# Two soft-MoE feed-forwards around an attention stage, fp32 in parts: a DMA pair moved ahead of a store, the last dispatch by halves, and first parts and slot outputs made earlier and on another engine

## The reference

```
x = x + 0.5 * ffn(layernorm(x))
x = x + attn(layernorm(x))
x = x + 0.5 * ffn(layernorm(x))
```

```
x = layernorm(x, norm_g, norm_b);  se = layernorm(slot_embeds) * scale
logits   = einsum("bnd,esd->bnes", x, se)
dispatch = softmax(logits, over tokens n);  combine = softmax(logits, over all 1024 slots)
slots = einsum("bnd,bnes->besd", x, dispatch)
gate  = gelu(einsum("besd,edf->besf", slots, Wg) + bg);  up = einsum(..., Wu) + bu
eout  = einsum("besf,efo->beso", gate * up, Wd) + bd
out   = einsum("bns,bso->bno", combine, eout)
```

## Time and profile before

| | us |
|---|---|
| median of 3 runs | 1966.77 |
| lowest, highest | 1964.76, 1971.29 |
| profiled execution, its own time | 1972.29 |
| its span | 1970.6 |
| PE busy in it | 1826.4 (93%) |
| DVE, ACT, POOL busy | 1333.0, 1128.0, 830.8 |
| mean granted TensorE clock | 0.978 |

### The profile page before, as it was taken

The page is one execution under the profiler, slowest core; times in us unless marked ns, Lnnn a source line. Parts: engine busy times, 40 slices in busy tenths (PEclk is TensorE's granted clock), DMA queues, the critical chain, the costliest instruction groups (busy, mean ns, idle before and its releaser), DMA issues. The chain is left out here.

```text
span 1970.6 us, 35473 instructions
## 1 busy us (share of the span) xinstructions
PE 1826.4 (93%) x11720; PEld 1632.3 (83%) x11720; DVE 1333.0 (68%) x2397; ACT 1128.0 (57%) x2233; POOL 830.8 (42%) x1005
## 2 busy tenths in 40 slices
PE   1999999999999899959999969999999999989999
PEld 1878787888899899948999957887878889989998
DVE  5866566664788888835555458666666648888886
ACT  1666566556555677724434427565665655557775
POOL 1353433524676455412222213535343356654553
PEclk9999999999999899979999979999999999999999
DMA  2543234323465577721221136324332516546774
GB/s 65 214 171 150 96 149 150 122 96 115 156 212 173 177 257 261 263 81 53 69 71 64 43 112 251 141 95 160 138 145 85 177 57 220 199 153 229 259 263 162
DMA packets 106666, 298.20 MB, mean 151 GB/s; under 512 B 16257, under 2 KB 56321, under 8 KB 94273
## 3 DMA queue, kind: packets, MB, share of 16 engines
q1 hardware_dynamic: 106560, 296.88, 42.5%
HBM read 187.63 MB, written 109.22 MB: 151 GB/s over the span
## 5 line engine op out<-in xcount | busy, mean ns | idle before, releaser
L115 POOL TENSOR_TENSOR pool_carrier<-minus_half 128x1 f32<-128x1 f32 x220 | 59.3, 270 | 640.8 <-PE f1bank L845 165.7
L688 ACT ACTIVATE f1r_lt<-f1bank,slot_shift 128x512 f32<-128x512 f32 x128 | 88.0, 688 | 138.0 <-PE f1bank L816 138.0
L688 ACT ACTIVATE f2r_lt<-f2bank,slot_shift 128x512 f32<-128x512 f32 x128 | 88.1, 688 | 136.5 <-PE f2bank L816 136.4
L547 DVE TENSOR_TENSOR f1r_e_lo<-f1bank,f1r_e_hi 128x512 fp32r<-128x512 f32 x128 | 82.8, 685 | 88.4 <-ACT f1r_e_hi L770 88.3
L547 DVE TENSOR_TENSOR f2r_e_lo<-f2bank,f2r_e_hi 128x512 fp32r<-128x512 f32 x128 | 82.5, 685 | 85.4 <-ACT f2r_e_hi L770 85.0
L1470 PE MATMUL f1bank<-f1c_eo,f1c_e_hi 128*128 128x258 f32 (+1 forms) x512 | 132.5, 290 | 3.4 <-DVE f1c_eo L1387 3.4
L1470 PE MATMUL f2bank<-f2c_eo,f2c_e_hi 128*128 128x258 f32 (+1 forms) x512 | 131.5, 288 | 3.5 <-DVE f2c_eo L1387 3.4
L1471 PE MATMUL f1bank<-f1c_eo,f1c_e_hi 128*128 128x256 f32 (+1 forms) x512 | 130.6, 286 | 0.0
L1471 PE MATMUL f2bank<-f2c_eo,f2c_e_hi 128*128 128x256 f32 (+1 forms) x512 | 129.6, 284 | 0.0
L1342 POOL TENSOR_TENSOR f1c_e_lo<-f1c_lt,f1c_e_hi 128x512 fp32r<-128x512 f32 x64 | 83.0, 1297 | 94.0 <-ACT f1c_e_hi L1441 93.9
L1342 POOL TENSOR_TENSOR f2c_e_lo<-f2c_lt,f2c_e_hi 128x512 fp32r<-128x512 f32 x64 | 83.1, 1298 | 91.9 <-ACT f2c_e_hi L1441 91.8
(11 more groups left out here) (319 smaller groups left out, 6637.1 us busy)
## 6 DMA issues: line engine op xcount, KB each, us to landing
logits<-f1r_lt SPq DMA_DIRECT2D x16, 2048.0 KB, 7.3
f1c_lt<-logits SPq DMA_DIRECT2D x32, 1024.0 KB, 7.3
...
```

Of the source, the lines that this page charges most:

```text
L115: pool.tensor_tensor(c["pool_carrier"][:, col:col + 1], c["minus_half"][:, 0:1], c["minus_half"][:, 0:1], ALU.add)
L547: dve.tensor_tensor(e_lo[t % 2][:, h * BANK:(h + 1) * BANK], ps_t[h][:, :], rd(e_hi[t % 2][:, h * BANK:(h + 1) * BANK]), ALU.subtract).the ...
L688: act.activation(lt[:, g, sc, :], ps_l[sc % 2][:, :], ACT.Identity, bias=c["slot_shift"][:, sc:sc + 1]).then_inc(logit_out, 1)
```

## The change

1. SP, route: the DMA pair of the reciprocals (L388, L391) stands ahead of `store_xn` of the group two later, where both belong to the last group of a batch.
2. PE, route: the last two token tiles of the last batch are dispatched as (t2, h0), (t3, h0), (t2, h1), (t3, h1) instead of tile by tile, and a wait for `e_lo` is left out at the last tile.
3. ACT makes `hi_g` and `hi_u` of the second expert (`second_gate_up`) ahead of the last slots' shifts. DVE makes `lo_g` of the second expert and `in_lo` of the first (`first_in_lo`) between the two halves of the last scaling.
4. DVE, experts: `in_lo` of the next expert stands behind the four gated products instead of ahead of them. In the last expert the first shifts of the combine stage stand among the gated products, and the rows of expert 14 behind the third shift.
5. PE, experts: the last pair is written out behind the loop, with `first_spread` ahead of the last hidden products.
6. Combine: the first slot outputs, hi and lo, are made by POOL, seven of the eight ahead of its part in the stage, instead of by ACT and DVE.
7. An unused semaphore is left out.

The core of the diff:

```diff
@@ route, SP
-                if fill and exists(b, g, 2):
-                    store_xn(i + 2, g % 2, b + (g + 2) // NG, (g + 2) % NG)
                 if drain and g == NG - 1:
 
                     sp.wait_ge(inv_done, b)
...
                     sp.dma_start(inv_rows[:, :], inv_dram.rearrange("(a n) -> a n", a=1).to_broadcast([P, SL]))\
                       .then_inc(inv_loaded, DMA)
+                if fill and exists(b, g, 2):
+                    store_xn(i + 2, g % 2, b + (g + 2) // NG, (g + 2) % NG)
@@ route, DVE, in the loop over halves h of the scaling
+                            if h == 0 and not fill:
+                                experts.first_in_lo(dve)
@@ route, ACT, ahead of the last slots' shifts
+        act.wait_ge(e_tr, 1 + HB * GT * B * NG)
+        experts.second_gate_up(act)
@@ route, PE
-                        pe.wait_ge(e_lo_done, 1 + HB * (GT * j + t + 1))
+                        if not (not fill and g == NG - 1 and t == GT - 1):
+                            pe.wait_ge(e_lo_done, 1 + HB * (GT * j + t + 1))
...
-                        dispatch(b, g, j, t)
+                        if not fill and g == NG - 1 and t >= GT - 2:
+                            if t == GT - 2:
+                                pe.wait_ge(xs_done, 1 + GT * j + t + 1)
+                                dispatch_half(b, g, j, t, 0)
+                            else:
+                                pe.wait_ge(xs_done, 1 + GT * j + t + 1)
+                                dispatch_half(b, g, j, t, 0)
+                                dispatch_half(b, g, j, t - 1, 1)
+                                dispatch_half(b, g, j, t, 1)
+                        else:
+                            dispatch(b, g, j, t)
@@ experts
+    def second_gate_up(act):
+        act.wait_ge(gate_up_loaded[1], 2 * DMA)
+        for n in "gu":
+            act.activation(hi[n][1][:, :, :], raw[n][1][:, :, :], ACT.Copy).then_inc(gate_up_hi, 1)
...
+    def first_in_lo(dve):
+        gate_parts_lo(dve, 1, 1)
+        slots_lo(dve, 0, 0)
@@ experts, DVE
-                if not (last and q == 1):
-                    parts_lo(e + 1, 1 - q)
+                if not (last and q == 1) and not (first and q == 0):
+                    gate_parts_lo(dve, e + 1, 1 - q)
+                if first and q == 0:
+                    slots_lo(dve, e + 1, 1 - q)
...
+                    if last and q == 1 and f < 2:
+                        combine.first_shifts(dve, f, f + 1)
+                if not (last and q == 1) and not (first and q == 0):
+                    slots_lo(dve, e + 1, 1 - q)
                 dve.wait_ge(h_hi_done, e + 1)
...
-                if not (first and q == 0):
+                if not (first and q == 0) and not (last and q == 1):
                     rows_out(e - 1, pair - 1 + q, 1 - q)
...
-        combine.first_shifts(dve)
+        combine.first_shifts(dve, 2, 3)
+        rows_out(E - 2, E // 2 - 1, 0)
+        combine.first_shifts(dve, 3, 4)
         rows_out(E - 1, E // 2 - 1, 1)
@@ combine, POOL
+        def first_slot_out(sc):
+            pool_wait(pool, c, experts["eout_done"], 1 + 2 * B * (sc + 1))
+            pool.tensor_scalar(eo[:, 0, sc, 0:D], eout[:, 0, sc, :], 1.0, 0.0, ALU.mult, ALU.add).then_inc(eo_hi_first, 1)
+            pool.wait_ge(eo_hi_first, sc + 1)
+            pool.tensor_tensor(eo[:, 0, sc, LO:W], eout[:, 0, sc, :], rd(eo[:, 0, sc, 0:D]),
+                               ALU.subtract).then_inc(eo_first, 1)
...
+        for sc in range(NSC - 1):
+            first_slot_out(sc)
```

More of the change, by code:

```diff
@@ L1016, in slots_hi, with slots_lo, gate_parts_lo @@
                        ACT.Copy).then_inc(in_hi_done, 1)
+    def slots_lo(dve, e, q):
+        dve.wait_ge(in_hi_done, e + 1)
+        for k in range(KD):
+            last = dve.tensor_tensor(in_lo[q][:, k, :].rearrange("p (b s) -> p b s", s=S), slots[:, k, e, :, :],
+                                     rd(in_hi[q][:, k, :]).rearrange("p (b s) -> p b s", s=S), ALU.subtract)
+        last.then_inc(in_lo_done, 1)
+    def second_gate_up(act):
+        act.wait_ge(gate_up_loaded[1], 2 * DMA)
+        for n in "gu":
+            act.activation(hi[n][1][:, :, :], raw[n][1][:, :, :], ACT.Copy).then_inc(gate_up_hi, 1)
+    def gate_parts_lo(dve, e, q):
+        dve.wait_ge(gate_up_hi, 2 * e - 1)
+        dve.tensor_tensor(lo["g"][q][:, :, :], raw["g"][q][:, :, :], rd(hi["g"][q][:, :, :]), ALU.subtract).then_inc(gate_lo, 1)
+    def first_in_lo(dve):
+        gate_parts_lo(dve, 1, 1)
+        slots_lo(dve, 0, 0)
     def first_in_hi(act):
@@ L1068, in act_program, with weights_hi @@
     def act_program(act):
-        def weights_hi(e, pair, q, first):
+        def weights_hi(e, pair, q):
             act.wait_ge(gate_up_loaded[q], 2 * DMA * (pair + 1))
-            if not first:
-                act.wait_ge(hidden_mm, KF * (e - 1))
+            act.wait_ge(hidden_mm, KF * (e - 1))
             for n in "gu":
@@ L1194, in pe_program, with emit @@
         down(0, 0, True)
-        with pe.Fori(1, E // 2) as pair:
+        def emit(pair, last):
             hidden(2 * pair, 0, False)
             down(2 * pair - 1, 1, False)
+            if last:
+                combine.first_spread(pe)
             hidden(2 * pair + 1, 1, False)
             down(2 * pair, 0, False)
-        combine.first_spread(pe)
+        with pe.Fori(1, E // 2 - 1) as pair:
+            emit(pair, False)
+        emit(E // 2 - 1, True)
         down(E - 1, 1, False)
-    return FirstExpert(load_first, first_gate_up, first_up_lo, first_down, first_in_hi), \
+    return FirstExpert(load_first, first_gate_up, first_up_lo, first_down, first_in_hi, first_in_lo, second_gate_up), \
         (sp_program, pool_program, dve_program, act_program, pe_program)
@@ L1278, in shift, with first_shifts @@
         dve.tensor_tensor(lt[par][:, sc, :], lt[par][:, sc, :], ps_r[par][:, :], ALU.add).then_inc(shifted, 1)
-    def first_shifts(dve):
-        for sc in range(FIRST):
+    def first_shifts(dve, begin, end):
+        for sc in range(begin, end):
             shift(dve, 0, 0, sc)
@@ L1411, in act_program @@
     def act_program(act):
-        def first_out_hi(sc):
-            act.wait_ge(experts["eout_done"], 1 + 2 * B * (sc + 1))
-            act.activation(eo[:, 0, sc, 0:D], eout[:, 0, sc, :], ACT.Copy).then_inc(eo_hi_first, 1)
         def slot_out_hi(b, par, sc):
@@ L1423, in exponential @@
                 k = BY_DVE.index(sc)
-                if first and k < 2:
+                if first and k == 1:
                     act.wait_ge(experts["eout_done"], 1 + B * (E - 1))
-                else:
+                elif not (first and k == 0):
                     act.wait_ge(lo_by_dve, len(BY_DVE) * n + k - 1)
```

38 lines of the change are left out of this document (11 added, 27 removed).

## The result

The changed kernel takes 1933.97 us (median of 4 runs, 1931.73 to 1935.21) against 1967.42 us before (1964.76 to 1971.29): a ratio of 0.9823, with a 95% interval of 0.9808 to 0.9839. The forecast was 1942, with a range of 1930 to 1957. The profiled execution of the changed kernel has a span of 1931.9 us, 38.7 less than the one before; part of this surplus over the medians is that the profiled run of before was one of its slower ones.

A forecast was written before the change was run, and what follows sets the result against it. PE was taken as the bound, busy 1826.4 of 1970.6 us. Terms of 13.5 - 5.7 + 5 + 11.4 = 24.2 us led from the median of 1966.8 to 1942.6, rounded to 1942; range 1930 to 1957.

The forecast's parts named there:

- three kinds of places: PE's waits at route batch ends, inside the experts for the gated product, and on either side of the expert stage.
- Part 1: Route batch ends: reciprocals' DMA pair issued 4.8 us earlier, removing 10.5 us of waits and 3.1 of clock; gain 13.5 us.
- The store that is late in exchange: Route, SP: the normalized group's store leaves at about 1325 instead of 1319.20; costed at nothing.
- Part 2: Route to experts: dispatch by halves, but `lo_u` blocks `in_lo`, so PE starts 0.75 us later; cost 5.7 us with clock.
- the 3 us named as a sign: Entry to the experts: an idle stretch of 3 us or more before the first hidden product would show the forecast cost.
- Part 3: Experts: `in_lo` moved into DVE's 1.13 us wait for `h_hi`; gain 5 us, bounds 0 and 10.6.
- Part 4: Experts to combine: first slot outputs on GpSimd remove PE's 3.44 us wait, plus clock; gain 11.4 us in all.
- the 2.3 us of clock at each place: First combine group: two thirds of the 3.4 us lost to lowered clock, counted as gained in each feed-forward.
- The entry not blocked: Entry to the experts: `in_lo` falls before `lo_u`, a gain of 4.5 us instead of a cost; 1932, chance 0.15.
- DVE and GpSimd eating parts 3 and 4: Experts and combine: the order in the experts gives 0, the exit only 6.9 us; 1952, chance 0.20.
- The early DMA moving nothing: Route batch ends: something else holds PE or landing takes longer, so the 13.5 us are lost; 1956, chance 0.08.
- The slower case: Experts: the moved `in_lo` is shut out in every expert, taking 2.60 us; 12.2 us slower, 1979, chance 0.05.

The follow-up runs named there:

- Part 1 alone: Kernel before with only the DMA pair of the reciprocals put ahead of the store of a normalized group: 1955.45 us, ratio 0.9924.
- part 4 alone: Kernel before with only the first slot outputs on GpSimd, DVE's new order in the last expert and the last pair written out: 1967.11 us, ratio 0.9985.
- part 3 undone: Changed kernel with `in_lo` ahead of the gated products again: 1948.92 us, ratio 0.9899 to the kernel before.
- the change with part 4 undone: Changed kernel without its changes from experts to combine, the others kept: 1941.66 us, ratio 0.9855 to the kernel before.

## Why the prediction was right, and where it was wrong

**What bounds the kernel.** Right: PE, with waits that DVE ended at three kinds of places, and a clock that made some of them dearer. All three kinds went or changed as named. One reading was loose: of the large waits said to lie in the setup and the attention stage, two (13.3 and 9.9 us, L803) stand at the start of the route stages. They are not touched either.

**Part 1, 13.5 us: right.** Part 1 alone measured 15.0 (12 to 18), 13.6 of it in the route stages; that is over the high bound of 13.6, which lies inside the interval. The store that is late in exchange cost nothing: the one wait for the load behind it (0.9 us, GpSimd in f1) is gone in the change.

**Part 2, a cost of 5.7 us: the mechanism right, the size wrong.** `in_lo` was shut out by `lo_u`, 2.43 us, and PE started later, by 0.3 instead of 0.75 us; with `lo_u` made to wait, `in_lo` took 0.76 us and PE's wait fell to 1.21. (Two details: in the earlier trace rows `in_lo` ended 0.6 us behind `lo_u`, not with it, and the idle stretch of 2.89 us stays just under the 3 us named as a sign.) The step that failed is the clock: I charged 1.7 + 2.5 us more for it, by analogy with the idle stretch of 3.44 us ahead of the combine stage. In the changed kernel the clock was lowered behind one of two entries, for 3.4 us, as before, so the term is 0. The earlier `lo_g` also took away a stall of 1.1 us at f1's second expert, which I had counted under part 3 only. Together: +1.4 us (-0.4 to 3.3) instead of -5.7.

**Part 3, 5 us of a possible 10.6: mis-sized by most of the error.** It measured 14.4 alone and 15 in the change. The step that failed: "`h_lo` would end about 0.5 us later: 0.25 of the 0.75 stays." I let GpSimd's `lo_d` hold `in_lo` and kept the hold of `h_lo` besides. The hold was not paid twice: `h_lo` behind the held `in_lo` runs free (1.23 us), and the hold moved to `lo_g`, which has slack. The upper bound of 10.6 was also low: it added up idle times, and from start to start each stop costs 0.16 us more.

**Part 4, 11.4 us: the exit right, a new wait missed.** It measured 3.0 alone and 6.3 on top of the others. The 3.44 us went twice, as forecast. The step that failed is "PE then goes from the last down product straight into L1470": it does, but the last `h_lo` comes late ahead of it, a wait that my sum had at nothing. It was 2.8 us in each feed-forward with part 4 alone, where the expert stages grew by 6.1 us in all, 2.8 and 2.9 with part 3 undone, and 0.7 in the change. Of the 2.3 us of clock at each place the runs show both more and less. Against the kernel before, part 4 alone shortens the combine stages by 3.6 and 1.4 us, 5.0 where 4.6 was summed. Against the change with part 4 undone it is only 1.1 and 0.7 us, since behind the same 3.4 us of idle time the clock was lowered for 3.4 us at each place there, and for 10.2 and 6.8 us in the kernel before. What sets that length no run shows.

The Trainium skill ("Perfetto Trace Analysis", section "Optimizing Scalar/DVE Operations") warns that moving work between DVE and GpSimd might not help, since they share a read port. The measured 6.3 us (7.5 for the move itself) are near the 6.9 that I had worked out for that case, but the trace bears its reason out only in one operation. GpSimd had stood idle there (11.52 us in the earlier trace rows), and in each feed-forward seven of the eight first subtractions ran at 0.64 to 0.74 us, as alone; one took 1.48, beside `h_lo` on DVE.

**The rivals.** The entry not blocked: not so in the change, and made so in the experiment with `lo_u` later, which gained 4.7 us of the 10.2 I had put on it. Its total, 1932, is nearer to the measured 1934 than mine is, but by no merit of its mechanism. DVE and GpSimd eating parts 3 and 4: no. The early DMA moving nothing: no. The slower case: the 2.60 us in every expert did not come, yet its logic of a DVE cycle was incomplete, as the experiment with `in_lo` behind `h_lo` shows: what slows the kernel there is not the length of the cycle but the time from the last gated product to `in_lo`.

**How much was luck.** By the runs of single parts the terms are off by +1.5, +7.1, +9.4 and -8.4 us. These add up to 9.6 us, because the miss in part 4 cancels most of one of the others. The range held by this cancelling as well as by its width.
